# First attention: the weighted sum's key tiles in one block, maxima and score tiles in turn behind it

## Chip, cores and metric

The kernel runs on one core of a Trainium2 chip. The metric is the device time of one execution in microseconds. A core has TensorE (PE, matmuls; PEld is its weight load), VectorE (DVE), ScalarE (ACT), GpSimd (POOL) and SyncE (SP, which here only starts DMAs). Matmuls write to PSUM, which has eight banks of 512 float32 columns for each of 128 partitions.

## The reference

Four layers, each added to x, which is 4 batches of 512 tokens of 128 features: an attention over the tokens and a context of 32 rows (16 heads of 64), a mixture of 8 experts with one chosen, a second attention over the context (16 heads of 8), and a mixture with two chosen. The change lies in the first attention:

```python
q = lat @ Wq                                   # lat: normalised x, 512 tokens
kv = jnp.concatenate([x, lat], axis=1) @ Wkv   # x here: the context, 32 rows
k, v = jnp.split(kv, 2, axis=-1)
dots = jnp.einsum('bhid,bhjd->bhij', q, k) * scale
attn = jax.nn.softmax(dots, axis=-1)
out = jnp.einsum('bhij,bhjd->bhid', attn, v)
return out @ Wout
```

## The kernel before

The first attention works on pairs of heads: 4 batches of 8 pairs, 32 in all. Each pair has 512 keys, in four key tiles of 128 (KT), and 32 context keys that are treated apart, four pairs at a time.

Queries and keys are float32r, split in a high and a low part (QH, QL, KH, KL). The softmax needs each query's maximum ahead of the exp. So every pair has two kinds of tiles, and all of them cover both heads at once in two neighbouring banks:

- *Maxima tiles* t0 to t3 (`top`, L1569): scores from the high parts, queries on the partitions, one matmul for each head. VectorE takes the largest of each row (L1235). t4 (L1576) is the same for the context keys and smaller (L1237).
- `mt` (`max_turn`): VectorE combines the maxima (L1246), TensorE transposes them (L1583), and ScalarE copies them as a row, TOPROW (L824).
- *Score tiles* s0 to s3 (`scores`, L1602): keys on the partitions, four products for each head (high and low parts, minus the maximum). ScalarE takes the exp into PT (L838). GpSimd adds the four tiles of exps up (L671), and `rows` (L1664, with the context's exps L1670 in every fourth pair) sums over the keys.
- The *weighted sum* p0 to p3 (`pv`, L1634): plain float32 matmuls of V with PT, which gather in bank 6. After p3 ScalarE copies the result to OT (L851).

`qk` (L1407 to L1409) makes the next pair's queries and keys, with copies on ScalarE (QH, KH, QF: L815, L816, L819) and the low parts on VectorE (KL, QL: L1225, L1228). `one_over` takes the reciprocal of the sums in four steps O0 to O3 of 128 columns (L1255), `spread` (P0, P2) brings them to the partitions with a matmul (L1689) and a product on VectorE (L1267), and `out` (L1700) is the output projection.

The order is written out by hand as a list of names, ITERATION. Pass i of the loop makes the queries and keys, maxima and `mt` of pair i+1, the scores of pair i, the weighted sum of pair i-1, and `rows` of pair i-1 if i is even. All five engines walk this one list, each taking its own part of each step, in order. Other work has places in the list as well: `E A B C V D` carry the layer norms, the values of the next batch and the router of the next layer. D has the normalisation `a_out` (passes 1, 9, 17) or `r0_out` (12, 20, 28), on ScalarE with scale and bias that GpSimd prepares at A, `a_split` (3, 11, 19), `r0_turn` (13, 21, 29), `r0_run` (15, 23, 31) and the sending of rows, `r0_send` (16, 24), which are indirect DMAs from GpSimd (L635). The reciprocal steps stand in passes 5, 9, ... 29, `spread` and `out` in 6, 10, ... 30. The context's scores are in CS, its weighted sum in PC (L1651).

Banks 0 to 5 are three pairs that every step of TAKES_BANKS takes in turn (`order_a`, L406 to L409). Taking a pair means waiting (`claim`) until the reader of its last contents is done: VectorE's maxima for t, ScalarE's exp for s.

```python
order_a.append((name, a, 2 * (place % 3), 2))
place += name in TAKES_BANKS
...
release(mine, (s_max, TOPS_OF * i + c + 1))
...
release(mine, (s_exp, SCORED[name, a]))
```

Of the kernel before, what the change touches and what calls it, by code (L numbers as in the profile page):

```python
# [41 lines left out]
def build(nc, x, ctx, lnm_g, lnm_b, lnl_g, lnl_b, Wq, Wkv, Wout, rw, rb, w1, w2, cq, ckv, cc, Wr, Wg, Wu, Wd, out):  # L42
    B, S, D = x.shape
# [4 lines left out]
    E = rw.shape[1]  # L48
# [22 lines left out]
    with ExitStack() as stack:  # L71
# [39 lines left out]
        V = BIG[:, 1:3, :].rearrange("p k (t n) -> p k t n", t=KT)  # L111
# [143 lines left out]
        for b in range(B):  # L255
# [61 lines left out]


        ITERATION = (
            "E A B PC CA0 C CA1 O0 ADD CS V qk p0 p1 t0 s0 t1 p2 t2 D s1 t3 p3 t4 P0 P2 s2 s3 rows mt O1 OUT "  # L320
            "O2 O3").split()

        beside = [{} for _ in range(ALL + 1)]
# [1549 lines left out]
```

## Time and profile before

| | us |
|---|---|
| median of 3 runs | 792.72 |
| lowest, highest | 792.16, 794.59 |
| profiled execution, span | 798.2 |
| PE busy in the span | 713.8 (89%) |
| DVE busy | 491.6 (62%) |
| POOL busy | 378.2 (47%) |
| ACT busy | 366.9 (46%) |

The profile is of one execution, and its page gives the span of that execution and no other time of it. Busy time is the time in which an engine has an instruction in work. Matmuls are pipelined, so a matmul's recorded duration overlaps the next one's start: the pace is read from the distance of the starts. Behind an arrow, in brackets, stands the idle time ahead of an instruction and what ended it. The first attention lasts from about 20 us to about 520 us of the span.

### The profile page before, as it was taken

Reading aid. Unit: us, or ns where it says so; the run is one execution under the profiler, and the core shown is the slowest. Engines: PE = TensorE matmul, PEld = TensorE weight load, DVE = VectorE, ACT = ScalarE, POOL = GpSimd, SP = SyncE. Lnnn points to the kernel's source line nnn. Section 1 sums busy time; section 2 is a strip of 40 time slices with the busy share of each in tenths; the row PEclk is TensorE's granted clock in tenths of the full one; section 3 lists DMA queues with packets and bytes.
Section 4 is the critical chain, followed back from the end, with each engine's and each line's share of the span. In section 5 each row is a group of like instructions: output and inputs, shape, how many; then the busy total and the mean of one; then the engine's idle time right before and its main releaser. Section 6 shows DMA issues by size and latency. Waiting matters only on the chain.

```text
span 798.2 us, 13900 instructions
## 1 busy us (share of the span) xinstructions
PE 713.8 (89%) x4626; PEld 414.0 (52%) x4626; DVE 491.6 (62%) x1077; ACT 366.9 (46%) x572; POOL 378.2 (47%) x369
## 2 busy tenths in 40 slices
PE   4899999999999999999999999987995587659991
PEld 4655556545556545555545455454664244326660
DVE  4655484595594875675775666664442477746673
ACT  5465554564654553654554643432332543314440
POOL 6254453553563573464375454524222314765552
PEclk9999999999999999999999999999998688569996
DMA  9999999300000000000030004302111500122224
GB/s 235 163 161 160 158 160 157 43 1 1 1 2 1 6 10 1 1 1 2 1 119 1 1 1 106 119 18 58 36 39 56 174 2 28 37 72 67 81 69 177
DMA packets 69132, 50.45 MB, mean 63 GB/s; under 512 B 4068, under 2 KB 62312, under 8 KB 69064
## 3 DMA queue, kind: packets, MB, share of 16 engines
q1 hardware_dynamic: 65544, 42.30, 29.7%
q0 software_dynamic: 3520, 7.27, 2.8%
q8 instruction: 41, 0.67, 0.4%
q14 instruction: 27, 0.22, 0.1%
HBM read 20.07 MB, written 29.47 MB: 62 GB/s over the span
## 4 chain that ended last, share of the span: by engine, by line
PE 75%; DVE 8%; issue 6%; POOL 4%; ACT 3%; DMA 2%; another core or an unknown queue 1%; SPq 1%; DVEq 0%; POOLq 0%; ACTq 0%
PE PSUM L1602 14%; PE PSUM L1634 13%; PE PSUM L1444 7%; PE PSUM L1569 5%; PE PSUM L1469 4%; PE PSUM L1700 4%; PE PSUM L1403 4%; PE PSUM L1407 3%; PE PSUM L1409 2%; PE PSUM L1408 2%; PE PSUM L1583 2%; PE PSUM L1576 2%; PE PSUM L1620 2%; PE PSUM L1664 2%; POOL results_d L643 2%
## 5 line engine op out<-in xcount | busy, mean ns | idle before, releaser
L838 ACT ACTIVATE PT<-PSUM 128x1024 f32<-128x1024 f32 x128 | 128.7, 1025 | 134.2 <-PE PSUM L1602 133.9
L671 POOL TENSOR_TENSOR PSUMS<-PT 128x1024 f32<-128x1024 f32 x32 | 76.1, 2378 | 210.6 <-ACT PT L838 171.6
L671 POOL TENSOR_TENSOR PSUMS<-PSUMS,PT 128x1024 f32<-128x1024 f32 x62 | 149.7, 2415 | 16.6 <-ACT PT L838 9.7
L1235 DVE TENSOR_REDUCE TOPS<-PSUM 128x2 f32<-128x1024 f32 x128 | 152.0, 1220 | 7.4 <-PE PSUM L1569 7.0
L1634 PE MATMUL PSUM<-PT,BIG 128*64 128x512 f32 x512 | 130.6, 611 | 0.6 <-issue 0.6
L1444 PE MATMUL PSUM<-BIG,XGT 128*128 x170 | 86.5, 614 | 2.4 <-issue 1.6
L1225 DVE TENSOR_TENSOR KL<-PSUM,KH 128x512 fp32r<-128x512 f32 x32 | 22.1, 692 | 68.0 <-ACT KH L816 67.5
L1189 DVE TENSOR_TENSOR SIL<-SIL,PSUM 128x256 f32<-128x256 f32 (+1 forms) x62 | 32.1, 518 | 48.0 <-ACT SIL L758 45.4
L1569 PE MATMUL PSUM<-KH,QH 64*128 64x512 f32 x256 | 58.0, 449 | 3.9 <-DVE QL L1228 3.6
L1634 PEld LDWEIGHTS PSUM<-PT,BIG 128*64 128x64 f32 x512 | 28.4, 135 | 54.0 <-issue 52.5
L1602 PE MATMUL PSUM<-QH,KH 64*128 64x512 f32 x256 | 54.9, 424 | 1.0 <-DVE QL L1228 0.8
L1569 PEld LDWEIGHTS PSUM<-KH,QH 64*128 64x128 f32 x256 | 24.2, 183 | 59.2 <-DVE TOPS L1235 25.1
L758 ACT ACTIVATE SIL<-PSUM 128x256 f32<-128x256 f32 (+1 forms) x62 | 28.7, 463 | 55.1 <-PE PSUM L1444 43.5
L643 POOL DMA_INDIRECT results_d<-YS,IDX x39 | 37.4, 960 | 31.5 <-issue 20.4
L766 ACT ACTIVATE HIDT<-PSUM 128x256 f32<-128x256 f32 (+1 forms) x62 | 28.7, 463 | 51.3 <-PE PSUM L1403 43.0
L1602 PE MATMUL PSUM<-QL,KH 64*128 64x512 f32 x256 | 50.9, 390 | 0.0
L1602 PE MATMUL PSUM<-QH,KL 64*128 64x512 f32 x256 | 50.8, 390 | 0.0
L1602 PE MATMUL PSUM<-TOPROW,MINUS 64*128 64x512 f32 x256 | 50.7, 389 | 0.0
L643 POOL DMA_INDIRECT results_b<-YS,IDX x23 | 22.0, 956 | 47.1 <-DVE YS L1196 44.8
L1274 DVE TENSOR_TENSOR OT<-OT,PSUM 128x1024 f32<-128x1024 f32 x16 | 18.9, 1217 | 34.0 <-PE PSUM L1651 34.0
L1444 PEld LDWEIGHTS PSUM<-BIG,XGT 128*128 128x128 f32 x170 | 28.1, 195 | 15.4 <-issue 15.3
L635 POOL DMA_INDIRECT lists_d<-BIG,SLOT x28 | 27.3, 975 | 10.4 <-issue 9.4
(255 smaller groups left out, 1358.5 us busy)
## 6 DMA issues: line engine op xcount, KB each, us to landing
lists_d<-EMPTY SPq DMA_DIRECT2D x3, 2730.0 KB, 44.7
lists_b<-EMPTY SPq DMA_DIRECT2D x3, 2470.0 KB, 41.7
lists_d<-EMPTY SPq DMA_DIRECT2D x1, 2665.0 KB, 43.9
XG<-lists_d SPq DMA_DIRECT2D x39, 65.0 KB
lists_b<-EMPTY SPq DMA_DIRECT2D x1, 2405.0 KB, 20.6
BIG<-in_L_ffn_w SPq DMA_DIRECT2D x1, 2048.0 KB
W2ALL<-in_L_ffn_w SPq DMA_DIRECT2D x4, 512.0 KB, 6.1
PT<-results_d SPq DMA_DIRECT2D x8, 256.0 KB, 4.9
```

Source lines behind the costliest of these rows:

```text
L643: pool.indirect_dma_start(RES[which], bass.IndirectOffsetOnAxis(ap=IDX[:, g % 8:g % 8 + 1].bitcast(U32), axis=0), YS[:, g % 8, :], None).t ...
L671: pool.tensor_tensor(PSUMS[:, i % 2], PTT[:, i % 2, 0] if kt == 1 else PSUMS[:, i % 2], PTT[:, i % 2, kt], ALU.add).then_inc(s_ps, 1)
L838: act.activation(PTT[:, i % 2, kt], PSUM[:, place:place + 2, :], ACT.Exp, scale=DH ** -0.5).then_inc(s_exp, 1)
L1189: dve.tensor_tensor(sl, sl, up, ALU.mult).then_inc(s_hid, 1)
L1235: dve.tensor_reduce(TOPS[:, c, 0, :], PSUM[:, place:place + 2, :], AX.X, ALU.max).then_inc(s_max, 1)
L1403: last = pe.transpose(PSUM[:, bank, t * P:(t + 1) * P], src(t), IDENT[:, :])
L1444: last = pe.matmul(PSUM[:, bank + n, :], XGT[:, g % 3, :], weights[:, bass.ds(column[which][j], BANK)], start=True, stop=True)
L1469: last = pe.matmul(PSUM[:, bank, 0:D], HIDT[:, g % 2, f * P:(f + 1) * P], weights[:, f * D:][:, bass.ds(column[which][j], D)], start=f == ...
L1569: last = pe.matmul(PSUM[:, place + h, :], QH[r, i % 2, c * P:(c + 1) * P], KH[r, i % 2, :], start=True, stop=True)
L1602: last = pe.matmul(PSUM[:, place + h, :], lhs, rhs, start=step == 0, stop=step == 3)
L1634: last = pe.matmul(PSUM[DH * h:DH * h + DH, 6, :], V[:, b % 2, kt, cols], PTT[:, i % 2, kt, h, :], start=kt == 0, stop=kt == KT - 1)
L1700: last = pe.matmul(PSUM[:, place, t * P:(t + 1) * P], OT[:, (GROUP * a + c) % OTS, t * P:(t + 1) * P], WOUT[:, (GROUP * a + c) % PAIRS, :] ...
```

## The change

Only the order of the names changes. p0 to p3 stand together ahead of t0, s1 moves to behind t1, s2 to behind D, s3 to behind t3, so that t4, the spread and `rows` follow s3, and O1 stands ahead of `mt` instead of behind it. OT is still copied at p3, which is now ahead of the exp of s0. GpSimd's additions keep their place with s1, s2 and s3, and so the first of them now stands ahead of D.

```diff
         ITERATION = (
-            "E A B PC CA0 C CA1 O0 ADD CS V qk p0 p1 t0 s0 t1 p2 t2 D s1 t3 p3 t4 P0 P2 s2 s3 rows mt O1 OUT "
+            "E A B PC CA0 C CA1 O0 ADD CS V qk p0 p1 p2 p3 t0 s0 t1 s1 t2 D s2 t3 s3 t4 P0 P2 rows O1 mt OUT "
             "O2 O3").split()
```

## Rows read from the trace of the kernel before

**Rows 1.** Table of windows, 60 to 500 us: busy PE, PEld, DVE, ACT, POOL, granted clock.

```profile
60.00:500.00 440.00, 436.07 (x3018) 240.75 (x3018) 285.65 (x400) 229.35 (x317) 224.75 (x115) 1.00 0.28 42
```

**Rows 2.** Timeline of PE, pass 12: start, duration, instruction, out<-in, count.

```profile
204.80 0.39 PE L1409 MATMUL PSUM<-XTH,WL 128*128 128x512 f32 x1
205.12 1.94 PE L1634 MATMUL PSUM<-PT,BIG 128*64 128x512 f32 x8
206.99 0.50 PE L1569 MATMUL PSUM<-KH,QH 64*128 64x512 f32 x2
207.33 0.40 PE L1602 MATMUL PSUM<-QH,KH 64*128 64x512 f32 x2
...
208.26 0.40 PE L1569 MATMUL PSUM<-KH,QH 64*128 64x512 f32 x2
208.59 1.08 PE L1634 MATMUL PSUM<-PT,BIG 128*64 128x512 f32 x4
209.60 0.50 PE L1569 MATMUL PSUM<-KH,QH 64*128 64x512 f32 x2
209.94 0.39 PE L1602 MATMUL PSUM<-QH,KH 64*128 64x512 f32 x2
...
212.20 0.62 PE L1576 MATMUL PSUM<-KCH,QH 64*128 64x32 f32 x8
212.67 0.47 PE L1602 MATMUL PSUM<-QH,KH 64*128 64x512 f32 x2
...
214.69 1.06 PE L1664 MATMUL PSUM<-PSUMS,ROWS_F 128*32 128x512 f32 x8
```

**Rows 3.** Timeline of PE, end of the stage: the last pair's weighted sum.

```profile
511.70 3.65 PE L1634 MATMUL PSUM<-PT,BIG 128*64 128x512 f32 x16
```

**Rows 4.** Waits of PE, 50 to 580 us: total, times, longest.

```profile
PE PSUM L1569 <- DVE QL L1228: 3.6, 5, 0.7
```

**Rows 5.** Timeline of DVE, passes 12 and 13.

```profile
210.14 2.38 DVE L1235 TENSOR_REDUCE TOPS<-PSUM 128x2 f32<-128x1024 f32 x2 [0.22 <-PE PSUM L1569]
...
230.25 2.56 DVE L1255 RECIPROCAL REC<-REC 64x128 f32<-64x128 f32 x3
```

**Rows 6.** Timeline of ACT, pass 12: exp, normalisations.

```profile
208.47 1.02 ACT L838 ACTIVATE PT<-PSUM 128x1024 f32<-128x1024 f32 x1 [1.67 <-PE PSUM L1602]
209.39 1.64 ACT L732 ACTIVATE NRM<-X,NMR,RSTD 128x128 f32<-128x128 f32 x4
```

**Rows 7.** Timeline of PE, start-up, where mt follows t4 at once.

```profile
24.63 0.62 PE L1576 MATMUL PSUM<-KCH,QH 64*128 64x32 f32 x8
26.06 0.63 PE L1583 MATMUL PSUM<-IDENT,TOPT 128*128 128x128 f32 x4 [0.82 <-DVE TOPT L1246]
```

**Rows 8.** Timeline of DVE, start-up: the combination of the maxima.

```profile
25.75 0.17 DVE L1246 TENSOR_REDUCE TOPT<-TOPS 128x8 f32<-128x16 f32 x1
```

**Rows 9.** Timeline of PE, pass 28: a score tile that waits for an exp.

```profile
459.00 0.50 PE L1602 MATMUL PSUM<-QH,KH 64*128 64x512 f32 x2 [0.29 <-ACT PT L838]
```

**Rows 10.** Timeline of ACT, pass 28: that exp.

```profile
457.86 1.00 ACT L838 ACTIVATE PT<-PSUM 128x1024 f32<-128x1024 f32 x1
```

**Rows 11.** Timeline, pass 22: the spread matmuls.

```profile
367.22 1.20 PE L1689 MATMUL PSUM<-RECS,SPREAD 128*128 128x512 f32 x4
```

**Rows 12.** The same timeline: the two products and the combination on DVE.

```profile
367.99 2.35 DVE L1267 TENSOR_TENSOR OT<-OT,PSUM 128x1024 f32<-128x1024 f32 x2 [0.23 <-PE PSUM L1689]
...
370.26 0.17 DVE L1246 TENSOR_REDUCE TOPT<-TOPS 128x8 f32<-128x16 f32 x1
```

**Rows 13.** Groups of instructions of POOL, 60 to 580 us: count, busy, mean ns, idle before.

```profile
L671 POOL TENSOR_TENSOR PSUMS<-PSUMS,PT 128x1024 f32<-128x1024 f32 x58 | 140.2, 2417 | 12.5 <-ACT PT L838 5.9 <-POOL PSUMS L671 0.4
...
L635 POOL DMA_INDIRECT lists_b<-NRM,SLOT x16 | 16.0, 1003 | 17.4 <-DVE NRM L1071 13.6 <-issue 3.8
```

**Rows 14.** Table of windows behind the first attention, columns as in rows 1.

```profile
540.00:560.00 20.00, 15.79 (x81) 10.33 (x82) 9.08 (x36) 5.16 (x9) 8.57 (x9) 1.00 0.21 58
...
600.00:620.00 20.00, 10.13 (x65) 7.61 (x63) 6.32 (x21) 4.12 (x7) 5.61 (x7) 0.82 0.25 79
```

## The prediction

> **What bounds the kernel now.** I read the table of windows first, for the 440 us in which the first attention runs: TensorE is busy 436.07 us of them at a granted clock of 1.00 (2.4 GHz), VectorE 285.65, ScalarE 229.35 and GpSimd 224.75 [rows 1]. TensorE sets the time; whatever it gains or waits there moves the end by the same amount, as nothing behind this stage has another start. Then I read TensorE's timeline of one pass of the loop (pass i handles scores of pair i, maxima of pair i+1, the weighted sum of pair i-1), and the timelines of VectorE and ScalarE beside it, to see how long after a tile's matmuls its reader is done with the banks. The reader is to see that no row of rows 2 has an idle time behind it: each consumer finishes while TensorE does other work. The weighted sum is that other work.
>
> **What the change gives.** The weighted-sum matmuls (L1634) are plain float32, their neighbours L1569 and L1602 are float32r. Each block of them costs more than its matmuls. From the start of the last neighbour ahead to the start of the second behind it: 204.80 to 207.33 = 2.53 us for a block of 8, and 208.26 to 209.94 = 1.68 for a block of 4 [rows 2]. Taking off the two neighbours at 0.23 each leaves 2.07 and 1.22, so four more matmuls cost 0.85 and a block itself 0.37. One block of 16 instead of 8+4+4 saves 2 x 0.37 = 0.74 us a pass. The tail of the stage shows a block of 16: 3.65 us against 1.94 + 1.08 + 1.08 = 4.10 [rows 2, 3]; that is 0.45 of it, the rest is the slow first step at either border (0.34 instead of 0.23). 31 passes: 22.9 us saved. A further 3.6 us go: five waits of maxima for QL [rows 4] end, since the block ahead of t0 is longer by 8 matmuls (1.7 us) and each wait was 0.75 at most.
>
> **What it costs, 1: the alternation.** Score and maxima tiles take three pairs of banks in turn, so each tile waits until the tile three places before it is read. Before, the sequence was t0 s0 t1 t2 s1 t3 t4 s2 s3 with blocks between; now t0 s0 t1 s1 t2 s2 t3 s3 t4 with nothing between: s1 needs t0's banks, t2 those of s0, and so on. Terms: t to its successor 0.34 behind a block or behind a wait, else 0.23; s to its successor 0.93 [rows 2]; VectorE starts 0.54 behind such a t (209.60 to 210.14), 0.44 behind another, and takes 1.22 [rows 2, 5]; ScalarE starts 0.04 behind the last score matmul's end, that is 1.14 behind the start of s, and takes 1.02 [rows 6]; TensorE starts 0.14 behind either engine's end [rows 7 to 10], I take 0.15. With t0 at zero:
> - s0 0.34, t1 1.27. s1 would start at 1.50, but t0's maxima end at 0.54 + 1.22 = 1.76, so s1 starts at 1.91.
> - t2 2.94; s2 3.17 (t1's maxima end at 2.93, so just in time); t3 would start at 4.10, but the exp of s1 runs from 3.15 to 4.17, so 4.32.
> - s3 would start at 4.66, the maxima of t2 end at 4.60, so 4.75; t4 5.79.
> Without waits t4 would start at 4.75. Lost: 1.0 us a pass, 31 passes with maxima: 31 us. Bounds: 0.7 (shorter releases) to 1.2.
>
> **Cost 2: the turn of the maxima (mt).** It needs t4's maxima and their combination on VectorE. Before, s2 and s3 (2 us) stood between. Now only `rows` does (about 1.0 us, 1.06 busy [rows 2]), and only in even passes. The start-up has the bare sequence: t4 at 24.63, mt at 26.06, 1.43 us [rows 7]; its last wait is the combination's, which ends at 25.92 [rows 8]. Unhindered, t4's successor comes 0.47 behind it [rows 2]. So 0.96 in each of the 16 passes without `rows` (0 and the odd ones to 29): 15.4 us. With `rows` between, the wait is gone.
>
> **Cost 3: the one reciprocal step.** O1 now stands ahead of the combination on VectorE in 7 passes (5, 9, ... 29), all odd, so nothing hides it. Three reciprocals take 2.56 us, a pitch of 0.81 to 0.85 [rows 5]: 7 x 0.84 = 5.9 us. Queued behind it are the combination, mt, the copy of the top row, and the next pass's projection. O2 and O3 have slack.
>
> **Cost 4: spread (P0, P2), 7 even passes.** It now follows t4. P2's banks wait for the exp of s3, about 0.3. On VectorE two products run ahead of the combination: it starts 370.26 - 367.22 = 3.04 behind P0's start in the trace [rows 11, 12]. With P0 at 6.34, P2 at 7.1 and `rows` at 7.7, mt could start at 8.8 but the combination ends near 9.5: 0.8. Less 0.15 that this place waits today: 7 x 0.95 = 6.7 us. Between 0 and 10.
>
> **Cost 5: other work at D.** D stood between t2 and s1, and now stands between t2 and s2. On ScalarE four normalisations (1.64 us) follow the exp of s1, so the exp of s2 ends 1.5 later and t4 waits for it: about 1.15 in six passes (1, 9, 17, 12, 20, 28), 6.9 us. Before, the weighted sum's block covered them: they start at 209.39 and the next banks to wait for came later [rows 2, 6]. GpSimd normally has its reciprocal roots ready by then. Feature splits, `r0_turn` and `r0_run` there (8 passes, a bank turn more or about 1 us of VectorE) I put at 1.8 us in sum, between 0 and 5. The sending of rows (`r0_send`, four indirect DMAs of about 1 us each, passes 16 and 24) falls on GpSimd behind the first addition of key tiles (2.4 us) [rows 13], which in even passes waits for `rows`: it is issued some 8 to 9 us later. Its first reader is ScalarE's normalisation in pass 17, a pass of 15 us later, and the exp of pass 18 behind the late additions; both have slack of about 1 us or more by my count, so zero, at worst 3. SP's queue and the remaining lists are not touched.
>
> **The sum.** -22.9 - 3.6 + 31 + 15.4 + 5.9 + 6.7 + 6.9 + 1.8 = +41.2 us on the profiled execution, whose span is 798.2; the page gives no other time of it. The median of the runs shown is 792.72, 5.5 lower, a difference that I carry over: 792.7 + 41 = 834. I predict 833.
>
> **Rivals.**
> - *The waits don't come, only the gain does.* If each release came before the bank is wanted, the result is 792.7 - 26.5 = 766, faster. It decides at 26.5 / 31 = 0.85 us of waits a pass; I count over 2. Against it: t0's maxima alone need 1.76 us and s1 wants the banks at 1.50 [rows 2, 5]. The Trainium skill, "Perfetto Trace Analysis", section "Matmuls", says that groups which rotate through PSUM banks let the reading of one overlap the matmuls of the next. By that rule this rival would hold; the trace agrees only where a block stands between. Chance 4%.
> - *Only the tail waits.* If the alternation ran at TensorE's pace but mt waited as counted, the sum is -26.5 + 15.4 + 5.9 + 6.7 = +1.5: 794. It would need VectorE to read a tile in under 0.9 us. Chance 5%.
> - *Only the alternation waits*, mt is somehow covered: -26.5 + 31 + 6.9 + 1.8 = +13: 806. The start-up's 0.96 speaks against it [rows 7]. Chance 5%.
> - *The block costs nothing itself*, so that nothing is saved (the change doesn't do what it says): 834 + 23 = 857. The block of 16 in rows 3 speaks against it. Chance 3%.
> - *The clock falls.* Waits of 1 to 2 us in nearly each pass leave TensorE about 90% busy. Between 540 and 560 us it was busy 15.79 of 20 us and the granted clock stayed 1.00; between 600 and 620, busy 10.13, it was 0.82 [rows 14]. Had the stage a mean of 0.95, its 436 us of work would grow by 23: 857. The Trainium skill, "TensorE: Matmul & The Clock Gate", section "A second HAM failure mode: psum-queue depth-cycling", describes just such short idles between groups that cycle through banks, with the clock swinging between its two levels. By it this case would be the likely one; rows 14 speak against it. Chance 5%.
>
> **How the numbers follow.** All terms as counted: 78%, 818 to 846. Its width: 31 passes x 0.2 is 6, the costs 4 and 5 another 8. To leave out no more than 2 in 10 the range must reach the third rival's 806 and a little above the counted case: 805 to 852. It leaves out 766, 794 and 857, 17% together. Chances: slower by over 0.3% (2.4 us, about what a measurement here can tell from no change) 0.92; within it 0.03 (the second rival, in part); faster 0.05.
>
> **What would show it.** In the profile after: one L1634 row of x16 a pass near 3.65 us; TensorE idle ahead of L1602 for VectorE's maxima (about 0.4, s1) and ahead of L1569 for ScalarE's exp (about 0.2, t3) in each pass; idle ahead of L1583 for the combination, 0.8 to 0.9 in odd passes, 1.7 where O1 stands; none where `rows` stands without spread. Granted clock 1.00 up to 540 us. TensorE's busy share in the stage near 91%. The prediction is wrong if the waits ahead of L1602 and L1569 sum to under 15 us, or if mt finds its maxima combined in odd passes.

## The result and the profile after

The changed kernel takes 854.8 us (median of 4 runs, 852.6 to 858.3) where the kernel before takes 793.7 (4 runs, 792.2 to 794.7): ratio 1.077, 95% interval 1.073 to 1.080. That is 61 us more; the forecast was 41 more, and its upper end, 852, is missed by 3. The sign was right, the size was not.

The table of windows of the changed kernel: the loop between the `mt` of pass 0 and that of pass 30, then passes 3, 4, 14 and 22 (a pass is counted from one `mt` to the next). Columns as in [rows 1].

```profile
42.44:555.42 512.98, 464.35 (x3052) 272.98 (x3053) 313.88 (x407) 242.38 (x332) 228.70 (x118) 0.96 0.30 42
68.91:85.98 17.07, 13.99 (x114) 7.83 (x111) 9.79 (x10) 8.31 (x11) 11.75 (x5) 0.97 1.31 147
85.98:103.66 17.68, 17.39 (x92) 10.39 (x92) 6.72 (x8) 7.90 (x10) 2.75 (x2) 0.83 1.22 148
...
256.56:273.92 17.36, 16.15 (x101) 9.70 (x101) 12.37 (x17) 8.54 (x11) 3.28 (x3) 1.00 0.00 1
...
401.67:422.18 20.51, 19.29 (x100) 11.86 (x101) 12.36 (x17) 8.53 (x11) 3.25 (x3) 0.83 0.01 1
```

Before, the same loop took 451.6 us, so 61.4 of the extra time lie in it and nothing behind it. (The two profiled spans differ by 55.8 only: what lies behind the loop takes 305.1 us in before's execution and 298.6 in this one. The change doesn't touch that part.) Two things are to be seen. TensorE is busy 464 of 513 us, that is 91%, the share that was forecast. But the granted clock, 1.00 throughout in [rows 1], is 0.96, and not evenly: 19 of the 30 passes have 1.00, three have 0.96 or 0.97 and eight have 0.82 to 0.91. Pass 4 is busy 17.39 us of 17.68 and waits for almost nothing; it is long because its matmuls run part of the time at 1.2 instead of 2.4 GHz. This low stretch lasts from 85.0 to 91.8 us; just before it, in pass 3, TensorE waited 2.67 us ahead of `mt`.

The waits of TensorE in the changed kernel, 30 to 600 us: waited for, total, times, longest.

```profile
PE PSUM L1583 <- DVE TOPT L1246: 28.6, 23, 2.7
PE PSUM L1602 <- DVE TOPS L1235: 7.6, 30, 0.3
PE PSUM L1576 <- ACT PT L838: 4.9, 6, 0.8
PE PSUM L1602 <- DVE PLACE L1050: 3.9, 2, 2.0
PE PSUM L1602 <- ACT PT L838: 2.0, 5, 0.4
```

The first row is `mt` waiting for the combined maxima; 23 times is the 16 passes without `rows` and the 7 with the spread, as counted. The second is s1 waiting for the maxima of t0, in each pass. The third is t4 in the six passes with normalisations. The QL waits of [rows 4] are gone. The fourth row, 2.0 us in each of two passes, was not in the forecast, nor was the longest wait of the first.

TensorE's timeline of the changed kernel, pass 11:

```profile
210.54 0.40 PE L1409 MATMUL PSUM<-XTH,WL 128*128 128x512 f32 x1
210.87 3.65 PE L1634 MATMUL PSUM<-PT,BIG 128*64 128x512 f32 x16
214.45 0.50 PE L1569 MATMUL PSUM<-KH,QH 64*128 64x512 f32 x2
214.79 0.39 PE L1602 MATMUL PSUM<-QH,KH 64*128 64x512 f32 x2
...
215.72 0.39 PE L1569 MATMUL PSUM<-KH,QH 64*128 64x512 f32 x2
216.36 0.50 PE L1602 MATMUL PSUM<-QH,KH 64*128 64x512 f32 x2 [0.26 <-DVE TOPS L1235]
...
218.76 0.50 PE L1569 MATMUL PSUM<-KH,QH 64*128 64x512 f32 x2
219.20 0.50 PE L1602 MATMUL PSUM<-QH,KH 64*128 64x512 f32 x2
...
220.20 0.61 PE L1576 MATMUL PSUM<-KCH,QH 64*128 64x32 f32 x8
223.45 0.63 PE L1583 MATMUL PSUM<-IDENT,TOPT 128*128 128x128 f32 x4 [2.63 <-DVE TOPT L1246]
```

Counted from t0 at 214.45, s1 stands at 1.91 (forecast 1.91), t3 at 4.31 (4.32), s3 at 4.75 (4.75), t4 at 5.75 (5.79). The bracket ahead of s1 says 0.26, but t1 to s1 is 0.64 where 0.23 would do, a loss of 0.41: as starts follow each other faster than ends, the first 0.16 of such a wait (0.39 recorded, 0.23 to the next start) doesn't show as idle time. So a sum of brackets is too low a price for many short waits. The block of 16, from its last neighbour ahead to the second start behind, takes 214.79 - 210.54 = 4.25; 2.53 for the block of 8 of [rows 2] and eight more matmuls at 0.85 for four make 4.23.

What the forecast had not is in the last row. In pass 11 `mt` waits 2.63 us, not 0.9. VectorE and GpSimd at that place:

```profile
219.17 2.46 DVE L935 TENSOR_TENSOR XTL<-XT,XTH 128x512 fp32r<-128x512 f32 x1
221.55 1.21 DVE L1235 TENSOR_REDUCE TOPS<-PSUM 128x2 f32<-128x1024 f32 x1
```

```profile
218.70 2.38 POOL L671 TENSOR_TENSOR PSUMS<-PT 128x1024 f32<-128x1024 f32 x1 [9.08 <-ACT PT L838]
221.23 5.14 POOL L671 TENSOR_TENSOR PSUMS<-PSUMS,PT 128x1024 f32<-128x1024 f32 x2
```

L935, the feature split at D, took 0.68 us before, when GpSimd was idle. Now GpSimd's first addition has been moved ahead of it with s1, and it is done only behind the end of the addition (221.08). The second row is a maximum from PSUM beside the next additions, and keeps its 1.2 us. The same place in pass 3 of the kernel before:

```profile
76.92 0.68 DVE L935 TENSOR_TENSOR XTL<-XT,XTH 128x512 fp32r<-128x512 f32 x1
```

```profile
77.80 2.39 POOL L671 TENSOR_TENSOR PSUMS<-PT 128x1024 f32<-128x1024 f32 x1 [3.85 <-ACT PT L838]
```

It is so in passes 3, 11 and 19. In passes 15 and 23 an instruction of a 128x32 tile (L1029), with both inputs in SBUF too, goes from 0.18 to 2.15 us beside such an addition, and TensorE waits 1.95 for what follows it (L1050).

### The profile page after: what moved, and what is told of

The parts are those of the page before. It is cut to its first block and busy times, and to the rows that moved or that the text cites. A ratio compares the mean times of both kernels' runs of the same rounds, so it can differ in the third digit from the quotient of the medians.

```text
span 854.0 us, 13900 instructions
## 1 busy us (share of the span) xinstructions
PE 725.9 (85%) x4626; PEld 441.6 (52%) x4626; DVE 516.5 (60%) x1077; ACT 370.2 (43%) x572; POOL 377.5 (44%) x369
## 5 line engine op out<-in xcount | busy, mean ns | idle before, releaser
L1634 PE MATMUL PSUM<-PT,BIG 128*64 128x512 f32 x512 | 120.8, 615 | 0.0
L1634 PEld LDWEIGHTS PSUM<-PT,BIG 128*64 128x64 f32 x512 | 34.9, 142 | 72.0 <-issue 70.5
L1602 PE MATMUL PSUM<-QH,KH 64*128 64x512 f32 x256 | 58.8, 441 | 13.6 <-DVE TOPS L1235 7.6
L1602 PE MATMUL PSUM<-QL,KH 64*128 64x512 f32 x256 | 53.6, 393 | 0.0
L1602 PE MATMUL PSUM<-TOPROW,MINUS 64*128 64x512 f32 x256 | 53.5, 392 | 0.0
L1602 PE MATMUL PSUM<-QH,KL 64*128 64x512 f32 x256 | 53.4, 392 | 0.0
L851 ACT ACTIVATE OT<-PSUM 128x512 f32<-128x512 f32 x32 | 19.2, 599 | 70.0 <-PE PSUM L1634 70.0
L824 ACT ACTIVATE TOPROW<-PSUM 128x512 fp32r<-128x512 f32 x32 | 19.1, 598 | 66.3 <-PE PSUM L1583 66.3
L1583 PE MATMUL PSUM<-IDENT,TOPT 128*128 128x128 f32 x128 | 22.2, 300 | 29.4 <-DVE TOPT L1246 29.4
L1602 PEld LDWEIGHTS PSUM<-QH,KH 64*128 64x128 f32 x256 | 26.7, 184 | 37.9 <-DVE TOPS L1235 26.0
L1569 PEld LDWEIGHTS PSUM<-KH,QH 64*128 64x128 f32 x256 | 25.8, 183 | 39.5 <-issue 25.1
```

Of the source, the lines that this page charges most:

```text
L1569: last = pe.matmul(PSUM[:, place + h, :], QH[r, i % 2, c * P:(c + 1) * P], KH[r, i % 2, :], start=True, stop=True)
L1583: last = pe.transpose(PSUM[:, place, t * P:(t + 1) * P], TOPT[:, 16 * t:16 * t + P], IDENT[:, :])
L1602: last = pe.matmul(PSUM[:, place + h, :], lhs, rhs, start=step == 0, stop=step == 3)
L1634: last = pe.matmul(PSUM[DH * h:DH * h + DH, 6, :], V[:, b % 2, kt, cols], PTT[:, i % 2, kt, h, :], start=kt == 0, stop=kt == KT - 1)
```

## The experiments

All were timed in turns with the kernel before on the same chip; it took 795 to 801 us there, so ratios are compared. 1% is 8 us. "Loop" is the length between the `mt` of pass 0 and of pass 30, 451.6 before.

**The block alone.** The kernel before with only p2 and p3 moved up.

```diff
-            "... qk p0 p1 t0 s0 t1 p2 t2 D s1 t3 p3 t4 P0 P2 s2 s3 rows mt O1 OUT "
+            "... qk p0 p1 p2 p3 t0 s0 t1 t2 D s1 t3 t4 P0 P2 s2 s3 rows mt O1 OUT "
```

> The kernel before with one part of the change alone: the weighted sum's four key tiles in one block ahead of t0, everything else in the old order (t0 s0 t1 t2 s1 t3 t4 s2 s3 rows mt O1). By the theory of bank waits (each tile waits for the reader of the tile three places before) the block saves 0.74 us a pass, but t2 now waits 0.4 for t0's maxima, s1 0.4 for the exp of s0, t4 0.3 for the maxima of t2 and s2 0.25 for the exp of s1: 1.4 us. Net +0.65 a pass, less 3.6 us of waits for QL that end: about 809 (803 to 815). The tail of the maxima stays covered by s2 and s3. If the rival held that the block is all gain and only the uncovered tail costs, this kernel would be faster than before: about 767.

Measured: ratio 1.033 (1.029 to 1.038), loop 476.7, +25.1. Its waits of TensorE:

```profile
PE PSUM L1602 <- ACT PT L838: 10.8, 48, 0.3
PE PSUM L1569 <- DVE TOPS L1235: 7.5, 30, 0.3
```

That is above the range expected (by the ratio about 819, against 803 to 815). The sign was right, the price was 1.1 us a plain pass instead of 0.65. TensorE's timeline of this kernel, pass 12, from t1 on:

```profile
209.26 0.40 PE L1569 MATMUL PSUM<-KH,QH 64*128 64x512 f32 x2
209.90 0.50 PE L1569 MATMUL PSUM<-KH,QH 64*128 64x512 f32 x2 [0.25 <-DVE TOPS L1235]
210.63 0.50 PE L1602 MATMUL PSUM<-QH,KH 64*128 64x512 f32 x2 [0.22 <-ACT PT L838]
210.93 0.42 PE L1602 MATMUL PSUM<-QH,KL 64*128 64x512 f32 x2
...
211.63 0.42 PE L1569 MATMUL PSUM<-KH,QH 64*128 64x512 f32 x2
212.20 0.62 PE L1576 MATMUL PSUM<-KCH,QH 64*128 64x32 f32 x8
213.02 0.50 PE L1602 MATMUL PSUM<-QH,KH 64*128 64x512 f32 x2 [0.20 <-ACT PT L838]
```

Four tiles wait, though only three have a bracket: t2 stands 0.64 behind t1 where 0.23 would do, s1 0.73 behind t2 (0.31), t4 0.57 behind t3 (0.23), s2 0.82 behind t4 (0.46). That is 1.53 us, and the step behind each wait is 0.31 instead of 0.23, another 0.3; less 0.74 for the block it makes the 1.1. My expectation had these four waits at 1.4 in sum, and none of the slow steps. Passes 9, 17 and 25 are only 0.08 to 0.16 longer: before, they held a wait for QL, which is gone, and that gives about 1.0 us in each. Since the clock is 1.00 here in each pass, this loss has nothing to do with it: taking the weighted sum out from between the tiles costs 25 us even with everything else left in its place.

**The tail covered.** The changed kernel with t4 ahead of s3, and `mt` ahead of O1.

```diff
-            "... qk p0 p1 p2 p3 t0 s0 t1 s1 t2 D s2 t3 s3 t4 P0 P2 rows O1 mt OUT "
+            "... qk p0 p1 p2 p3 t0 s0 t1 s1 t2 D s2 t3 t4 s3 P0 P2 rows mt O1 OUT "
```

> The changed kernel with its alternation kept, but t4 ahead of s3 and O1 behind mt, so that s3 (1 us) covers the maxima's tail again. By the theory of bank waits: waits of about 1.4 us a pass in the alternation less 0.74 for the block, mt waits 0.2 at most, no single wait over 1 us but in few passes: about 810 (803 to 818), and a granted clock of 1.00 in the first attention. If the alternation itself pulled the clock down, it would stay near the changed kernel's 0.95 and the time above 825.

Measured: ratio 1.055 (1.050 to 1.060), loop +45.5, mean clock 0.97. By the ratio that is about 836, where I had 803 to 818 and a clock of 1.00: missed. Its waits:

```profile
PE PSUM L1602 <- ACT PT L838: 13.5, 18, 1.4
PE PSUM L1602 <- DVE TOPS L1235: 7.5, 30, 0.3
PE PSUM L1583 <- DVE TOPT L1246: 6.1, 3, 2.0
PE PSUM L1576 <- DVE PLACE L1050: 3.9, 2, 2.0
```

Where the clock is 1.00 and nothing stands at D, the passes are near what was expected: 0.6 to 0.7 us over the kernel before in even ones, 0.8 to 0.95 in odd ones (25, 29 and 30, whose wait for QL is gone, are not longer). The rest stands in other passes: 3, 11 and 19 are 3.0 us longer (the third row: `mt` waits 2.0 three times), 15 and 23 are 3.5 longer (the fourth), 12, 20 and 28 are 3.0 to 3.5 longer, where TensorE waits 1.4 for the exp behind the normalisations and the clock falls to 0.90, and 1, 2, 4, 16, 17, 18 and 24 are 1.1 to 2.2 longer, at clocks of 0.90 to 0.97. So this run pointed to two causes beside the counted waits: VectorE's instructions at D, and the clock.

**The reciprocal step back.** The changed kernel with `mt` ahead of O1.

```diff
-            "... t3 s3 t4 P0 P2 rows O1 mt OUT "
+            "... t3 s3 t4 P0 P2 rows mt O1 OUT "
```

> The changed kernel with the reciprocal step O1 behind mt again. Counted: 7 passes by 0.84 us = 6 us faster than the changed kernel, 849. If long single waits (1.8 us and more) are what lets the clock fall, passes 10, 18 and 22, behind O1, get their full clock back, another 6 us or so: about 843. If the clock falls for all the small waits together, only the 6 us.

Measured: ratio 1.071 (1.066 to 1.076), loop 504.6, 8.4 less than the changed kernel's. In the O1 passes that have a clock of 1.00 in both kernels (5, 13, 17, 21, 25, 29) the difference is 0.65 to 0.70 a pass; the forecast put 0.84. Seven of them are 4.8 us, and the rest of the 8.4 lies in passes whose clock differs between the two. The expectation for the clock held in part: passes 10 and 22 have 1.00 again, pass 18 has 0.90 as before, and passes 2, 12 and 14, which had 1.00, now have 0.88 to 0.91. The two ratios' intervals overlap, so it is the passes that show the price of O1 and not the time.

**O1 alone.** The kernel before with O1 ahead of `mt`, and so with s2 and s3 between t4 and it.

```diff
-            "... t4 P0 P2 s2 s3 rows mt O1 OUT "
+            "... t4 P0 P2 s2 s3 rows O1 mt OUT "
```

> The kernel before with one edit: O1 moved ahead of mt, with s2 and s3 still in front of it. My theory: two score tiles (1.9 us of TensorE) stand between t4 and mt, and the combination needs 0.96 us of VectorE plus 0.84 for the reciprocal, 1.8 in sum, so the step is just covered: ratio 0.999 to 1.002, and no wait ahead of mt above 0.3 us. Rival: the step costs its 0.84 us in each of 7 passes wherever it stands ahead of the combination: ratio 1.007 (about +6 us).

Measured: ratio 1.000 (0.997 to 1.003); no pass behind the first differs by more than 0.02 us. The same edit that costs 0.7 us a pass in the changed kernel costs nothing where two score tiles cover it.

**Unused matmuls in the waits, first try.** The changed kernel with matmuls whose result nobody reads, into bank 6 ahead of `mt`: 3 (7 with O1, 11 in passes 3, 11, 19).

```diff
                 elif name == "max_turn":
+                    i = a - 1
+                    if i >= 1:
+                        pe.wait_ge(s_const_r, 2)
+                        n = 11 if i in (3, 11, 19) else 7 if i % 4 == 1 and i > 4 else 3 if i % 4 == 2 or i % 2 else 0
+                        keep_busy(6, n)
                     pe.wait_ge(s_comb, a + 1)
```

If the clock falls because TensorE waits, filling the waits must make the kernel faster although it does more.

> The changed kernel with unused matmuls (0.21 us each, into bank 6, which is free there) in TensorE's wait ahead of mt: 3 in odd passes and where spread stands, 7 where O1 stands, 11 in passes 3, 11 and 19. No dependence is changed and the waits end when they ended. Theory of the clock: the changed kernel's time over the count of waits (about 20 us) is the clock that falls to 1.2 GHz behind idle stretches; with them filled the granted clock of the first attention goes from 0.95 to 1.00 and the time falls by 15 to 22 us, to about 835. Rival: the additional time is other work that became slower, and the clock's reading is a by-product: the time stays at 855 or rises by up to 5 us, since the unused matmuls come on top.

Measured: ratio 1.075 (1.071 to 1.080), no gain. The trace tells why: in passes 4, 10, 16, 18, 20, 22 and 24, where the changed kernel loses most, the excess over before fell from 22.4 to 8.1 us in sum; but passes 3, 11 and 19 grew by 2.0 to 3.3, since `mt` waits up to 2.1 us for its banks there, and the unused matmuls stood behind that wait instead of in it. So this run decided nothing by its time.

**Unused matmuls, second try.** The same, but each group ahead of the taking of the banks, and more of them.

```diff
+                unused = 0
+                if name == "max_turn" and a > 1:
+                    unused = 11 if a - 1 in (3, 11, 19) else 7 if (a - 1) % 4 == 1 and a > 5 else 3 if (a - 1) % 4 == 2 or a % 2 == 0 else 0
+                elif name == "scores" and a in ((15, 3), (23, 3)):
+                    unused = 8
+                elif name == "top" and a[1] == TOPS_OF - 1 and a[0] - 1 in (1, 9, 17, 12, 20, 28):
+                    unused = 3
+                if unused:
+                    pe.wait_ge(s_const_r, 2)
+                    keep_busy(6, unused)
                 if name in TAKES_BANKS:
                     claim(*mine)
```

> The changed kernel with the same unused matmuls as in the earlier kernel, but each group ahead of the claim of the banks, so that it lies inside the wait it is meant to fill, and further groups where that kernel still waited long: 11 in passes 3, 11 and 19, 8 ahead of s3 in passes 15 and 23, 3 ahead of t4 in the six normalisation passes. Theory (about 20 us of the excess over the kernel before are a clock that falls behind long waits): granted clock 0.99 or 1.00 in each pass of the loop, ratio 1.050 to 1.060, that is 13 to 20 us less than the changed kernel's 1.077, although TensorE does more work. Rival (the low clock records are a by-product and the waits alone cost the time): ratio 1.073 to 1.08.

Measured: ratio 1.058 (1.054 to 1.062). Windows of the loop and of passes 4 and 22:

```profile
43.88:540.63 496.75, 484.68 (x3207) 288.64 (x3208) 315.47 (x407) 242.83 (x332) 229.72 (x118) 1.00 0.29 43
88.20:103.17 14.97, 14.66 (x93) 8.40 (x92) 6.72 (x8) 7.91 (x10) 2.84 (x2) 1.00 1.23 160
...
392.47:409.80 17.33, 16.87 (x105) 10.10 (x103) 12.25 (x17) 8.54 (x11) 3.15 (x3) 1.00 0.01 1
```

The clock is 1.00 in each pass of the loop. Pass 4, with the work that it had, takes 14.97 us instead of 17.68, pass 22 takes 17.33 instead of 20.51. With 155 matmuls more in the trace of the loop, it is 16.2 us shorter. So the fall of the clock is a cost of its own, about 15 us by the ratios (1.077 - 1.058 = 0.019), and the waits bring it about: once they are filled it is gone. Not all of them: s1 still waits in each pass, 7.6 us in sum, and the clock stays at 1.00.

**GpSimd held back.** The changed kernel with one wait more: in passes 3, 11 and 19 the first addition starts behind L935.

```diff
+                    if kt == 1 and i in (3, 11, 19):
+                        pool.wait_ge(*XTD.at(i // PAIRS + 1, "low"))
                     pool.tensor_tensor(PSUMS[:, i % 2], PTT[:, i % 2, 0] if kt == 1 else PSUMS[:, i % 2], PTT[:, i % 2, kt],
```

> The changed kernel with one added wait: in passes 3, 11 and 19 GpSimd starts its first addition only when VectorE's product for the feature split at D (L935) is done. Theory (that product takes 2.46 us instead of 0.68 since it runs beside GpSimd's addition): L935 takes 0.68 again in these passes, the wait ahead of mt falls from 2.6 to about 0.9 us, each of the three passes is 1.5 to 1.8 us shorter, and the low clock behind them (passes 4 and 20 at least) comes back: ratio 1.065 to 1.071, 5 to 9 us less than the changed kernel's 1.077. Rival (the product is slow for another reason): L935 stays at 2.4 and the ratio at 1.077.

Measured: ratio 1.072 (1.067 to 1.076), just above the range expected; the interval reaches from inside it nearly to the changed kernel's 1.077, so the time alone would not decide. The trace does. Pass 11, VectorE and TensorE (line numbers are two higher here):

```profile
216.47 0.69 DVE L937 TENSOR_TENSOR XTL<-XT,XTH 128x512 fp32r<-128x512 f32 x1
```

```profile
218.98 0.63 PE L1585 MATMUL PSUM<-IDENT,TOPT 128*128 128x128 f32 x4 [0.86 <-DVE TOPT L1248]
```

0.69 instead of 2.46, and `mt` waits 0.86 instead of 2.63; each of the three passes is 1.75 to 1.78 us shorter. So L935 was long because of GpSimd's addition. The clock came back in passes 4 and 20, but fell in passes 2, 14 and 30, where it had been 1.00. Pass 14 of this kernel, whose order and waits are those of pass 14 of the changed kernel:

```profile
252.05:272.61 20.56, 19.35 (x100) 12.24 (x101) 12.35 (x17) 8.53 (x11) 3.24 (x3) 0.83 0.00 1
```

The row of the changed kernel, at the top, has 17.36 us at 1.00; this one 20.56 at 0.83. The same pass of the same program text costs 3.2 us more at the lower clock. Which pass is hit thus doesn't follow from its own waits alone, and my expectation that shorter waits in three passes would also win back clock in the sum failed: the length of the passes times what their clock lacks to 1.00 comes to 22.2 us in the changed kernel and 20.5 in this one. Nor does the length of one wait tell: in the changed kernel `mt` waits 2.6 to 2.7 us in each of passes 3, 11 and 19, and passes 4 and 20 behind it have 0.83 and 0.90, pass 12 has 1.00. Each kernel has one trace here, so whether the place also changes from one execution of a kernel to the next is not shown.

**Both taken away.** Unused matmuls as above (without those of passes 15 and 23 and the extra ones of 3, 11, 19), and GpSimd held back in passes 3, 11, 19 and also 15, 23, behind L1029. The part for GpSimd:

```diff
                     if kt == 1 and i in (3, 11, 19):
                         pool.wait_ge(*XTD.at(i // PAIRS + 1, "low"))
+                    if kt == 1 and i in (15, 23):
+                        pool.wait_ge(*RD0.at(i // PAIRS - 1, "diff"))
```

> The changed kernel with both suspected terms taken away at once: unused matmuls in the waits ahead of mt and of t4 (none in passes 15 and 23, and none beyond the plain number in 3, 11 and 19), and GpSimd's first addition held back until VectorE's instruction on SBUF is done (L935 in passes 3, 11, 19; L1029 in passes 15, 23). Theory (what my count lacked is a clock loss of 16 to 20 us and the meeting of VectorE and GpSimd with 8 to 10 us, and nothing else): clock 1.00 in all passes, L935 at 0.7 us, the loop between the mt of pass 0 and of pass 30 takes 34 to 40 us more than before, ratio 1.043 to 1.052, which is my forecast's +41 us (1.052) or a little less. Rival (a further term is missing in the count): ratio 1.058 or more.

Measured: ratio 1.047 (1.045 to 1.049), loop 487.6, +36.0, clock 1.00. The waits of TensorE:

```profile
PE PSUM L1614 <- DVE TOPS L1239: 7.6, 30, 0.3
PE PSUM L1614 <- ACT PT L842: 2.0, 5, 0.4
```

Of the changed kernel's five rows two are left, s1's in each pass and a short one for exps; the other three are filled or gone, but for 0.8 us ahead of the `mt` of pass 0. 1.047 is +37 us, within what was expected and near the forecast's 41: what the forecast counted, without what it had not counted. (A little over 1 us of it are the unused matmuls themselves, 0.2 in each O1 pass.)

**Another order.** The kernel before with score tiles in twos, and p3 beside `rows`.

```diff
-            "... qk p0 p1 t0 s0 t1 p2 t2 D s1 t3 p3 t4 P0 P2 s2 s3 rows mt O1 OUT "
+            "... qk p0 p1 t0 s0 s1 t1 p2 t2 D s2 s3 t3 t4 P0 P2 p3 rows mt O1 OUT "
```

> The kernel before in another order: p0 p1 t0 s0 s1 t1 p2 t2 D s2 s3 t3 t4 P0 P2 p3 rows mt O1 OUT. Two blocks of float32 are kept where they cover readers, and the third is laid beside rows, so that it has a border less where rows stands, and stands between t4 and mt where it covers the combination in the odd passes. Theory (a block costs 0.37 us, a wait is what it is by the count of bank turns): one block less in 16 even passes, less about 0.2 us a pass for t4, which wants the banks of s2: ratio 0.992 to 1.000. Rival: the waits for the exps of s2 and s3 are longer than counted, since two score tiles follow each other (1.0 us each on ScalarE against 0.93 on TensorE): ratio 1.005 to 1.02.

Measured: ratio 1.015 (1.012 to 1.018): slower, within what the rival gave. Even plain passes are unchanged (-0.01): p3 beside `rows` saves a border, and t4's wait for the exp of s2 and slower steps around it take it back. Plain odd ones are 0.33 longer, since p3 alone doesn't cover the combination. More of the loop's 10 us lies in the passes with other work: 10, 18 and 26, with the spread, are 1.0 longer each, and 15 and 23 0.9.

**mt apart.** The kernel before with the combination where it was, but `mt`'s transposes behind the next pass's qk, directly ahead of p0 (in the 23 places without context scores; the expectation has 24), and `rows` behind p3. In the list `turn` is the transposes and their row, `mt` the combination.

```diff
-            "... V qk p0 p1 t0 s0 t1 p2 t2 D s1 t3 p3 t4 P0 P2 s2 s3 rows mt O1 OUT "
+            "... V qk turn p0 p1 t0 s0 t1 p2 t2 D s1 t3 p3 rows t4 P0 P2 s2 s3 mt O1 OUT "
```

> The kernel before with mt taken apart: VectorE still combines the maxima behind t4, but TensorE's transposes (and ScalarE's row) stand behind qk of the next pass, directly ahead of p0 p1, in the passes that make no context scores (24 of 31); rows stands behind p3. Both are float32 beside float32, so that a block of float32 less is laid in those passes, and the combination has all of qk as further cover. Theory (each block of float32 costs 0.37 us whatever stands in it, and no reader is late): 24 x 0.37 = 8.9 us less, ratio 0.987 to 0.992. Rival (what a block costs is in the weighted sum's own 16 matmuls and not at its borders, or the copy of the top rows comes late for s0): ratio 0.998 to 1.01.

Measured: ratio 1.007 (1.005 to 1.009): slower, the rival. TensorE's timeline of this kernel, around one such place:

```profile
143.13 0.39 PE L1609 MATMUL PSUM<-TOPROW,MINUS 64*128 64x512 f32 x2
143.46 0.50 PE L1414 MATMUL PSUM<-XTH,WH 128*128 128x512 f32 x1
...
144.72 0.39 PE L1416 MATMUL PSUM<-XTH,WL 128*128 128x512 f32 x1
144.95 0.60 PE L1590 MATMUL PSUM<-IDENT,TOPT 128*128 128x128 f32 x4
145.48 1.94 PE L1641 MATMUL PSUM<-PT,BIG 128*64 128x512 f32 x8
```

L1609 and L1414 are both float32r, and yet the step between them is 0.33 instead of 0.23. L1416 is float32r and L1590 float32, and that step is 0.23. What changes in the first and not in the second is the shape of the weights (64*128 to 128*128). The other rows say the same. L1590 and L1641 are both float32, with weights of 128*128 and 128*64, and the step is 0.53. In the kernel before the same transposes stand ahead of qk, so that the type changes and the shape doesn't, and the step is 0.41:

```profile
449.05 0.66 PE L1583 MATMUL PSUM<-IDENT,TOPT 128*128 128x128 f32 x4
449.46 0.48 PE L1407 MATMUL PSUM<-XTH,WH 128*128 128x512 f32 x1
```

So the extra 0.1 at a border was not float32 beside float32r, as my count had it, but one shape of tile beside another. The Trainium skill, "TensorEngine Tiling (Array Packing)", section "Key Properties", says that a change of the tiling mode, as against one of the tile, drains TensorE; these rows agree, at 0.1 us for each change. `mt` between s3 and qk costs no more borders than `mt` between qk and p0, and nothing was to be gained. 6.6 us of waits for QL in 10 places (before, in the same window: 4.4 in 6) explain about half of what it lost. The rest is about 0.1 us in each pass: behind pass 27, where nothing waits, p0 starts 2.35 us behind the last score product instead of 2.30, and p2 3.54 behind p0 instead of 3.47.

None of the orders tried beats the kernel before.

## Why the prediction missed

The forecast failed because it had no term for two costs that the changed kernel has on top of the counted waits: VectorE's instructions beside GpSimd's additions, and the lower clock. By the ratios the 61 us are made up so: 37 remain with both causes taken away (0.047 x 794), 9 lie between that kernel and the one with filled waits alone (0.011), 15 between that and the changed kernel (0.019).

Point by point:

- *What the block gives*: 0.74 us a pass counted, right. The tiles' part of the pass can be read off: 4.25 us for one block against 2.53 + 1.68 + 1.68, less the four neighbours more (0.92) that the three windows hold, is 0.72. The reason was wrong: the price of a border belongs to the change of shape. It didn't matter here, as every border of these blocks is both; it misled the last experiment.
- *The alternation*: 1.0 us a pass, right to 0.04 (t4 at 5.75 instead of 5.79). The working took 1.03 from s1 to t2 and 1.04 from s3 to t4, though its list of terms has 0.93: the slow first step behind a wait, which the list gives for maxima tiles only. In pass 11 s3 to t4 took 1.00. With the block's gain this gives +0.26 for a plain even pass; passes 2 and 8 show +0.21 and +0.19.
- *The waits for QL*: 3.6 forecast, as the sum of the brackets. The kernel with the block alone gives about 1.0 us back in each of passes 9, 17 and 25 and 1.1 to 1.3 in 29 and 30, some 5 in sum. It is why pass 30, which has the spread, is only 0.28 longer in the changed kernel. This error made the forecast too high.
- *mt behind t4*: 0.96 in the passes without `rows`. Pass 27 is +1.12, less 0.20 for what the even ones have is 0.9: right.
- *Spread*: 0.95 over an even pass; passes 6, 14 and 26 show +1.24 to +1.26, less 0.20 is 1.05: right.
- *O1*: 0.84 forecast, 0.65 to 0.70 measured; `mt` waits 1.49 in these passes, where the forecast had 1.7.
- *Normalisations at D*: 1.15 forecast; pass 28 shows +0.84, pass 12 +1.29, and 0.20 of either is an even pass's own, so 0.6 to 1.1. Mis-sized, by some 2 us in the sum.
- *Other work at D*, 1.8 us between 0 and 5: the step that failed first. I priced VectorE's instructions there by their duration before, with GpSimd idle beside them, though I had written that GpSimd's first addition now stands ahead of D. In five passes it costs 1.75 to 1.95 us each, 9 us in all.
- *The clock*: the step that failed most. It was no term of the sum, but a rival that excluded the counted case, with 5%, and its price was taken for a mean of 0.95. The loop had 0.96, and it cost 15 us on top of the counted waits (16 by the length of the loops). I had let [rows 14] speak against it: 79% busy at 1.00. One window without a fall was weak evidence for 31 passes with waits. The Trainium skill, "TensorE: Matmul & The Clock Gate", section "A second HAM failure mode: psum-queue depth-cycling", which the forecast cited and set aside, describes what came: short idles between groups that cycle through banks, and a clock that swings. The runs agree with it so far that filling the idles ends the swing; but the kernel with the block alone has four waits of 0.34 to 0.42 us in most passes and keeps 1.00.

The counted case was 78% likely by my list and came out at +37; the truth was that case and two costs beside it. The errors of its own terms were small, 1 to 2 us each for QL, O1 and the normalisations, and these three lay on the same side: they are why it came out at 37 and not at 41. The range reached 852 because it took in only the errors of the terms. Costs that come on top of every case belong into the sum and into the range's upper end.

## What to carry to other kernels

Work that looks like a gap-filler between tiles (here the weighted sum in three pieces) may be the cover that lets three banks' readers catch up; merging it saves a border of a few tenths and uncovers a wait of more than that. When waits of 1 to 3 us are put into a TensorE stream that ran at full clock, price them twice: the wait itself, and a share of the passes at a lower granted clock (here 15 us on top of 46). And when a step is moved on one engine, look at what runs at that time on VectorE and GpSimd together: durations read from the old trace hold only for the old neighbours.

## What the runs showed of the hardware

- A VectorE instruction with both inputs in SBUF that starts beside a GpSimd addition of a 128x1024 tile ends only behind it: 2.46 us instead of 0.68 for 128x512, and 2.15 instead of 0.2 for 128x32, while VectorE's reductions from PSUM keep 1.2 us. The Trainium skill, "SBUF — State Buffer", section "Who interferes with whom", says that a VectorE instruction with two SBUF inputs contends with a GpSimd instruction that reads SBUF; the trace agrees.
- Matmuls nobody needs can make a kernel faster: 1.077 to 1.058 by keeping the granted clock at 1.00.
- The same pass with the same waits took 17.36 us at a granted clock of 1.00 and 20.56 at 0.83. Where the clock falls differs between the traces of these kernels, and what decides the place stays open.
- A change between 64*128, 128*128 and 128*64 weights costs TensorE about 0.1 us at the first step (0.33 instead of 0.23, and 0.53 instead of 0.41); one between float32r and float32 of the same shape doesn't (0.23).
